# Fewer matmuls for a per-batch rank product: high and low halves side by side, one group at a time, in a five-engine fp32 kernel

## The reference

```python
def _L0_cond_ref(x, adapter_mapping, W, b, lora_As, lora_Bs):
    base_out = jnp.einsum('bti,oi->bto', x, W) + b
    A = lora_As[adapter_mapping]      # (128, 512, 16)
    Bm = lora_Bs[adapter_mapping]     # (128, 16, 512)
    lora_h = jnp.einsum('bti,bir->btr', x, A)
    lora_out = jnp.einsum('btr,bro->bto', lora_h, Bm)
    return base_out + lora_out * SCALING

x = x + _L0_ffn_ref(_L0_cond_ref(x, ...), W_gate, W_up, W_down)   # silu(gate) * up, 1376 wide, then down
x = x + _L1_ffn_ref(_L1_cond_ref(x, ...), ...)                    # two routed low-rank layers
```

## Time and profile before

| what | value |
|---|---|
| three runs, median (lowest to highest) | 981.73 us (980.36 to 982.88) |
| the profiled execution, device time | 981.22 us |
| its span in the trace | 979.5 us |
| PE busy | 972.1 us (99%) |
| DVE / ACT / POOL busy | 586.0 / 464.5 / 276.9 us |

### The profile page before, as it was taken

How to read it: one execution, slowest core, us unless ns; L and a number is a source line. 1 busy time by engine, 2 the same in 40 slices (tenths; PEclk the granted TensorE clock), 3 DMA queues, 4 the chain that set the end, 5 groups by cost and what they waited for, 6 DMA issues and landing times.

```text
span 979.5 us, 14271 instructions
## 1 busy us (share of the span) xinstructions
PE 972.1 (99%) x4723; PEld 822.1 (84%) x4723; DVE 586.0 (60%) x970; ACT 464.5 (47%) x855; POOL 276.9 (28%) x284
## 2 busy tenths in 40 slices
PE   9999999999999999999999999999999999999998
PEld 7888888888888888888888888888888899898986
DVE  4545487876992432685423398333278488786862
ACT  4646476655742333571333383233357264545342
POOL 5363524654300721400522230261140460000000
PEclk9999999999999999999999999999999999999999
DMA  7899868686968866877886777987688650616132
GB/s 239 269 362 321 265 232 300 243 295 243 369 237 296 295 195 193 278 235 263 278 278 195 234 246 249 322 280 194 194 275 314 236 194 22 236 37 223 65 108 86
DMA packets 131123, 230.14 MB, mean 235 GB/s; under 512 B 29798, under 2 KB 29799, under 8 KB 130539
## 3 DMA queue, kind: packets, MB, share of 16 engines
q1 hardware_dynamic: 126720, 216.35, 66.4%
q0 software_dynamic: 4192, 12.87, 3.6%
q10 hardware_dynamic: 138, 0.01, 0.0%
HBM read 165.74 MB, written 63.44 MB: 234 GB/s over the span
## 4 chain that ended last, share of the span: by engine, by line
PE 87%; SPq 5%; DVE 2%; DMA 2%; issue 2%; ACT 1%; ACTq 0%; DVEq 0%
PE bank L1951 87%; SPq L597 3%; DMA x_raw<-in_x 1%; PE bank L2114 1%; SPq L583 1%; DMA c<-c_scratch 1%; SPq L588 0%; DMA a_raw<-in_a_cols 0%; SPq L664 0%; DVE xa_lo L1502 0%; ACT c_out L1076 0%; SPq L596 0%; ACT dt L1102 0%; SPq L772 0%; DVE hg L1762 0%
## 5 line engine op out<-in xcount | busy, mean ns | idle before, releaser
L1951 PE MATMUL bank<-cop_hi,wring 128*128 128x512 f32 x1234 | 380.9, 389 | 0.0
L1951 PEld LDWEIGHTS bank<-cop_hi,wring 128*128 128x128 f32 x1234 | 231.6, 188 | 48.8 <-DVE v L1590 0.4
L1951 PE MATMUL bank<-cop_lo,wring 128*128 128x512 f32 x616 | 239.7, 389 | 0.0
L1951 PE MATMUL bank<-op_hi,wring 128*128 128x512 f32 x560 | 173.8, 389 | 0.0
L1590 DVE TENSOR_TENSOR v<-bank,p7s 128x512 f32<-128x512 f32 x44 | 30.4, 691 | 194.0 <-PE bank L1951 193.9
L1951 PEld LDWEIGHTS bank<-cop_lo,wring 128*128 128x128 f32 x616 | 115.6, 188 | 24.0
L1951 PEld LDWEIGHTS bank<-op_hi,wring 128*128 128x128 f32 x560 | 105.1, 188 | 22.0 <-DMA wring<-wd_scratch 0.2
L1951 PE MATMUL bank<-op_lo,wring 128*128 128x512 f32 x280 | 108.9, 389 | 0.0
L1176 ACT ACTIVATE s<-bank 128x512 f32<-128x512 f32 x44 | 26.3, 597 | 112.6 <-PE bank L1951 112.6
L1576 DVE TENSOR_TENSOR op_lo<-h,op_hi 128x512 fp32r<-128x512 f32 x100 | 72.6, 743 | 3.7 <-ACT op_hi L1133 3.6
L909 POOL TENSOR_TENSOR h_t<-h,h 128x512 f32<-128x512 f32 x20 | 27.1, 1356 | 160.8 <-DVE h L1612 160.8
(11 more groups left out here) (243 smaller groups left out, 1925.8 us busy)
## 6 DMA issues: line engine op xcount, KB each, us to landing
wring<-wgu_scratch SPq DMA_DIRECT2D x231, 256.0 KB, 3.1
wring<-wd_scratch SPq DMA_DIRECT2D x140, 256.0 KB, 5.5
wgu_scratch<-wring SPq DMA_DIRECT2D x77, 256.0 KB, 3.5
c_scratch<-c_out POOLq DMA_DIRECT2D x32, 256.0 KB, 3.3
c<-c_scratch SPq DMA_DIRECT2D x32, 256.0 KB, 4.7
xs_raw<-x_scratch SPq DMA_DIRECT2D x16, 512.0 KB, 5.2
out<-res SPq DMA_DIRECT2D x32, 256.0 KB, 2.1
x_raw<-in_x SPq DMA_DIRECT2D x14, 512.0 KB, 5.8
```

Source lines behind the costliest of these rows:

```text
L1951: return e.matmul(out_ap, lhs, rhs, start=start, stop=stop, skip_group_check=True)
```

## The change

The weights of a group now hold, for each of two halves of 4 batches, 64 columns of high and 64 columns of low part of A (`a_both`; the order low, high, high, low lets one copy write all the high ones, and `a_place` puts the batches to suit). The moving operand is the high and low part of 128 tokens side by side, 256 columns (`xa` holds both). One matmul per chunk and half gives all four partial products, so the rank product has 2 x 2 x 4 = 16 matmuls of 256 columns. Each group has a bank of its own. Three of the four quarter results have to be added: ACT turns those that lie on the other 64 partitions (`lora_turn`, two copies into `h_turned`), DVE adds twice and then scales and masks (`lora_in`, three operations that depend on one another, 256 elements wide), ACT and DVE make high and low part per group. DVE's `a_lo` is two half-size operations per group. `h_turned` is cleared once at the start.

The first two tiles are woven anew by groups. `load_x(3)` moves from t = 1 to t = 0 on SP, `load_down` from t = 0, 1 to t = 1, 2. The 14 down steps stand four places later, in tiles 2 to 5. In tile 6 three `cop_split` stand ahead of the closings instead of six, and one follows each closing.

```diff
-    a_hi = work("a_hi", [NG, KC, P], F32R)
-    a_lo = work("a_lo", [NG, KC, P], F32R)
+    a_both = work("a_both", [NG, KC, 2 * P], F32R)
...
-    xa_hi = [work(f"xa_hi{s}", [KC, TOK], F32R) for s in range(2)]
-    xa_lo = [work(f"xa_lo{s}", [KC, TOK], F32R) for s in range(2)]
+    xa = [work(f"xa{s}", [2, KC, TOK], F32R) for s in range(2)]
...
+    h_turned = sb("h_turned", [NG, 2, GT // 2], F32, w_region + 8 * ROW)
...
-    c_ring = [("h", t, 0, "dve") for t in range(NT)]
+    c_ring = [("h", t, g, "dve") for t in range(NT) for g in range(NG)]
...
-    ring_bank_at = [3, 3] + [n % 4 for n in range(2, len(c_ring))] + [n % 4 for n in range(len(l_ring))]
+    ring_bank_at = [3] * 4 + [(n + 2) % 4 for n in range(len(c_ring) - 4)] + [n % 4 for n in range(len(l_ring))]
...
-    d_at = [KC + 1 + n for n in range(N_EARLY)]
+    d_at = [2 * KC + 1 + n for n in range(N_EARLY)]
...
+    HB, HR = GB // 2, P // 2
+    def a_views(g, b, at_col):
+        n = b.stop - b.start
+        return (a_both[:, g, :, at_col:at_col + n * R].rearrange("p k (b r) -> p k b r", b=n),
+                a_raw[:, g, b, :].rearrange("p b (k r) -> p k b r", k=KC))
+    def a_place(b):
+        return (b + HB) % GB
+    def h_n(t, g=NG - 1):
+        return NG * t + g + 1
+    def h_bank(t, g):
+        return ring_bank("h", t, g)[:, :].rearrange("p (w h c) -> p w h c", w=2, h=2)
+    def by_turn(ap):
+        return ap.rearrange("p (w c) -> p w c", w=2)
...
# SP
-            if t == 1:
+            if t == 0:
                 for ks in x_parts(3):
                     load_x(3, ks)
-            if t < 2:
-                load_down(t)
+            if 0 < t < 3:
+                load_down(t - 1)
...
# ACT
+        def lora_turn(t, g):
+            both = h_bank(t, g)
+            e.wait_ge(pe_ring, ring_full("h", t, g))
+            if t == 0:
+                e.wait_ge(dve_chain, ZEROS + 1)
+            else:
+                e.wait_ge(*ring_freed("h", t - 1, g))
+            e.activation(h_turned[0:HR, g, 0, :], both[HR:P, 0, 0, :], ACT.Copy).then_inc(h_turned_done, 1)
+            e.activation(h_turned[HR:P, g, 1, :], both[0:HR, 1, 0, :], ACT.Copy).then_inc(h_turned_done, 1)
...
-        lora_in(0)
-        turn_a(1)
+        turn_b(0)
+        for g in range(NG):
+            lora_turn(0, g)
+            lora_hi(0, g)
+        turn_a(1, (0,))
+        lora_turn(1, 0)
...
-        for m in close_order(0):
-            close_c(0, m)
+        close_c(0, 0)
+        turn_a(1, (1,))
+        close_c(0, 1)
+        lora_hi(1, 0)
+        close_c(0, 2)
+        close_c(0, 3)
+        turn_b(1)
+        lora_turn(1, 1)
+        split_x(2, (0, 1))
+        lora_hi(1, 1)
+        split_x(2, (2, 3))
...
-            for q, i in cop_due(t)[:6]:
+            ahead = 3 if t == NT - 2 else 6
+            for q, i in cop_due(t)[:ahead]:
                 cop_split(0, q, i)
             for r, m in enumerate(close_order(t)):
                 close_c(t, m)
                 for n in d_due(t, r):
                     down_hi(n)
-            for q, i in cop_due(t)[6:]:
-                cop_split(0, q, i)
+                if t == NT - 2:
+                    for q, i in cop_due(t)[ahead + r:ahead + r + 1]:
+                        cop_split(0, q, i)
+            if t == NT - 1:
+                for q, i in cop_due(t)[ahead:]:
+                    cop_split(0, q, i)
...
# DVE
-            e.scalar_tensor_tensor(
-                out=h_masked[:, :].rearrange("p (g c) -> p g c", g=NG),
-                in0=ring_bank("h", t, 0)[:, :].rearrange("p (g c) -> p g c", g=NG), scalar=SCALING,
-                in1=own_batch[:, :].unsqueeze(1).to_broadcast([P, NG, GT]),
-                op0=ALU.mult, op1=ALU.mult).then_inc(dve_freed, 1)
+            linked(e.tensor_tensor(by_turn(mine), both[:, :, 0, :], h_turned[:, g, :, :], ALU.add))
+            e.wait_ge(dve_chain, links[0])
+            linked(e.tensor_tensor(by_turn(mine), both[:, :, 1, :], by_turn(mine), ALU.add))
+            e.wait_ge(dve_chain, links[0])
+            e.scalar_tensor_tensor(out=mine, in0=mine, scalar=SCALING, in1=own_batch[:, :],
+                                   op0=ALU.mult, op1=ALU.mult).then_inc(dve_freed, 1)
...
# PE
-            for g in range(NG):
-                e.wait_ge(a_lo_done, NG * t + g + 1)
+            e.wait_ge(a_lo_done, h_n(t, g))
+            for w in range(2):
+                at_tok = g * GT + w * GT // 2
+                first = P if w == 0 else 0
                 for k in range(KC):
-                    if g == 0:
+                    if g == 0 and w == 0:
                         e.wait_ge(x_lo, x_n(t, k))
-                    tok = slice(g * GT, (g + 1) * GT)
-                    done = mm3(bank[:, tok], a_hi[:, g, k, :], a_lo[:, g, k, :],
-                               xa_hi[s][:, k, tok], xa_lo[s][:, k, tok], k == 0, k == KC - 1)
+                    done = mm(by_turn(bank[:, w * GT:(w + 1) * GT]), a_both[:, g, k, first:first + P],
+                              xa[t % 2][:, :, k, at_tok:at_tok + GT // 2], k == 0, k == KC - 1)
...
-        lora_out(0)
-        lora_in(1)
+        lora_out_half(0, 0)
+        lora_in(1, 0)
+        lora_out_half(0, 1)
         e.wait_ge(c_closed, c_turn(0, 0))
-        for k in range(KC):
-            cond_base(1, KC - 1, k)
-        lora_out(1)
+        cond_base(1, KC - 1, 0)
+        cond_base(1, KC - 1, 1)
+        lora_in(1, 1)
+        cond_base(1, KC - 1, 2)
+        cond_base(1, KC - 1, 3)
+        lora_out_half(1, 0)
+        lora_out_half(1, 1)
```

More of the change, by code:

```diff
@@ L102, in build @@
     lh_lo = [work(f"lh_lo{s}", [TOK], F32R) for s in range(2)]
-    xa_hi = [work(f"xa_hi{s}", [KC, TOK], F32R) for s in range(2)]
-    xa_lo = [work(f"xa_lo{s}", [KC, TOK], F32R) for s in range(2)]
+    xa = [work(f"xa{s}", [2, KC, TOK], F32R) for s in range(2)]
+    xa_hi, xa_lo = ([xa[s][:, half, :, :] for s in range(2)] for half in range(2))
     h_masked = work("h_masked", [TOK], F32)
@@ L390, in build @@
     IDENT, MASK, LATER, EXPERT = 3, 6, 8, 9
-    ZEROS, ROWS = 1, 4
+    ZEROS, ROWS = 1, 5
     def x_parts(t):
@@ L1047, in split_w0, with turn_a @@
             e.activation(w0_hi[:, k, :], w0_raw[:, k, :], ACT.Copy).then_inc(w0_hi_done, 1)
-        def turn_a(t):
-            for g in range(NG):
+        def turn_a(t, gs=range(NG)):
+            for g in gs:
                 if (t, g) == (0, 1):
@@ L1533, in lora_in @@
-            e.wait_ge(lh_hi_done, t + 1)
-            e.tensor_tensor(lh_lo[t % 2][:, :], h_masked[:, :], plain(lh_hi[t % 2][:, :]),
+            if t > 0:
+                e.wait_ge(lh_lo_done, h_n(t - 1, g))
+            linked(e.tensor_tensor(by_turn(mine), both[:, :, 0, :], h_turned[:, g, :, :], ALU.add))
[4 more added lines that the diff above has]
+                                   op0=ALU.mult, op1=ALU.mult).then_inc(dve_freed, 1)
@@ L1535, in lora_in, with lora_rest @@
+        def lora_rest(t, g):
+            tok = slice(g * GT, (g + 1) * GT)
+            e.wait_ge(lh_hi_done, h_n(t, g))
+            e.tensor_tensor(lh_lo[t % 2][:, tok], h_masked[:, tok], plain(lh_hi[t % 2][:, tok]),
                             ALU.subtract).then_inc(lh_lo_done, 1)
@@ L1796, in dve_program @@
         turn_a(0)
-        lora_in(0)
-        turn_a(1)
+        turn_b(0)
+        for g in range(NG):
+            lora_in(0, g)
+            lora_rest(0, g)
+        turn_a(1, (0,))
+        lora_in(1, 0)
+        turn_a(1, (1,))
+        lora_rest(1, 0)
+        turn_b(1)
+        lora_in(1, 1)
+        split_x(2, (0, 1))
+        lora_rest(1, 1)
+        split_x(2, (2, 3))
         for t in range(1, NT):
-            if t == 1:
-                split_x(2, (0, 1))
-            else:
+            if t > 1:
                 turn_a(t)
+                turn_b(t)
                 if t < NT - 1:
                     split_x(t + 1)
-            if t == NT - 1:
-                for n in range(7):
-                    gate_up_lo(n)
-                cop_begin(0, 1)
-            lora_in(t)
-            if t == 1:
-                split_x(2, (2, 3))
+                if t == NT - 1:
+                    for n in range(7):
+                        gate_up_lo(n)
+                    cop_begin(0, 1)
+                for g in range(NG):
+                    lora_in(t, g)
+                for g in range(NG):
+                    lora_rest(t, g)
             if t == NT - 2:
@@ L1993, in cond_base, with cond_lora @@
                 xa_hi[t % 2][:, k, :], xa_lo[t % 2][:, k, :], k == 0, False)
-        def cond_lora(t, m):
+        def cond_lora(t, m, g):
             s = t % 2
-            for g in range(NG):
-                tok = slice(g * GT, (g + 1) * GT)
-                done = mm3(c_banks(t)[m][:, tok], b_hi[s][:, g, m * P:(m + 1) * P], b_lo[s][:, g, m * P:(m + 1) * P],
-                           lh_hi[s][:, tok], lh_lo[s][:, tok], False, g == NG - 1)
-            done.then_inc(pe_acc, 1)
+            tok = slice(g * GT, (g + 1) * GT)
```

(17 more changed lines are left out.)

111 lines of the change are left out of this document (60 added, 51 removed).

## The result

The changed kernel takes 985.59 us (median of 7 runs, 984.54 to 986.82) beside 981.73 us before (7 runs, 980.34 to 982.88): 1.0044 times, 95% interval 1.0033 to 1.0055 (such a ratio is worked out from all the runs and is not the quotient of the two medians). It is slower by 0.4%, where 980.6 [976.5 to 984.5] was forecast. The profiled execution took 986.48 us, its span 984.8. Of all executions behind this document one, of the later version back_and_lora, took 1975.54 us, and its ratio leaves it out.

What follows compares the result with a forecast made beforehand. The path feeding tile 7 (SP's issues, load of c, splits), not PE alone, was taken to decide. PE's 7.7 us, mostly lost to two waits, left 0.1 to 0.7; 1.1 was taken: 981.22 to 980.1, median 980.6 [976.5 to 984.5].

Steps and rivals of the forecast that it cites:

- PE's part: Rank product: eight fewer matmuls a tile, 0.12 us apart, save 0.96 us a tile, 7.7 in eight tiles.
- rival C: Rank product: the two-run read is slower, at 0.228 us a matmul 6 us in all, 988 us; chance 0.04.
- Tiles 0 and 1: First two tiles: about 2 us of waits in place of 0.9, tile 2 starts 0.85 us earlier, bounds 0 and 2.8.
- SP's queue: SP's gathers and loads: tile 4's gathers 3.3 us earlier, near 61; load_c starts at 110.8 for 113.19.
- the landing of that store: Tile 5's last store, issued at about 114.3, lands after the median 5.5 us, so cop_hi starts at 119.8.
- rival B: Stores of tile 5 come late and hold ACT's first cop_split; at 12.0 us of landing 988 us; chance 0.11.
- floor: Behind load_c: the last store lands no sooner than c itself, 118.2, and not at 117.4.
- Rival E: Expansion of tile 7: PE's pause ahead of it costs speed, some 1.7 us, ending at 982.3; chance 0.05.
- D: The prediction's own forecast for the whole kernel, 978.8 to 983 us; chance 0.50.
- better half: Whole kernel: a saving of 1.1 us was taken, where the middle values gave 0.1 to 0.7 and the best case 2.6.
- The end of tile 7: From c's data to the last lh_lo 4.74 us, 1.35 more than before; PE waits 3 to 3.6 us.
- Rival A: Path ahead of tile 7 is not the bound, PE keeps its saving: 975.2 to 976.7 us, near part 978; chance 0.30.

Runs made afterwards that it cites:

- back_and_lora: Changed kernel with down steps and their reads in the old tiles and DVE's cop_begin(0, 1) behind lora_in(7): 982.17 beside 981.11 us, 1.0005.
- Experiment 13: Changed kernel with each early down step storing 128 of its 512 columns: 981.47 beside 981.14 us, 1.0013.
- Experiment 7: Changed kernel with POOL's sums of down weights behind lh_lo of tiles 2 and 4: 984.84 beside 981.23 us, 1.0033.
- Experiments 9 to 12: clear_path (981.52 us), and clear_path with stores behind the next tile's first gathers (983.11), later down steps (982.52), or a quarter of early store bytes (976.75).
- clear_path: Changed kernel with down steps and reads in old tiles, POOL's sums after DVE's lora operations, cop_begin(0, 1) behind lora_in(7): 981.52 beside 981.23 us, 1.0001.
- filler: Changed kernel with ten unused matmuls of 512 columns ahead of the expansion of tile 7: 989.8 beside 981.23 us, 1.0082.
- experiments 3, 10 and 11: Changed kernel with tile 5's stores ahead of the first c load (986.27 us); clear_path with stores behind the next first gathers (983.11), or later down steps (982.52).
- experiment 14: clear_path with three down steps a tile in place of four, the last two stores behind c: 980.5 beside 981.74 us, 0.9991.
- steps_back: Changed kernel with the 14 down steps and the reads of down weights back in their old tiles: 981.98 beside 981.37 us, 1.0008.
- sums_clear: The run of Experiment 7, changed kernel with POOL's sums behind lh_lo of tiles 2 and 4: 984.84 beside 981.23 us, 1.0033.
- old_steps_late: Kernel before with only the changed kernel's late down steps, reads of down weights and early x read: 986.98 beside 981.37 us, 1.0061.
- stores_first: Changed kernel with SP issuing the three stores of tile 5 ahead of the first load of c: 986.27 beside 981.37 us, 1.0051.
- after_few_bytes: The run of Experiment 13, changed kernel with a quarter of the columns in the early down stores: 981.47 beside 981.14 us, 1.0013.
- lora_first: Changed kernel with DVE's cop_begin(0, 1) behind the lora operations of tile 7: 983.82 beside 981.37 us, 1.0027.
- old_lora_first: Kernel before with DVE's cop_begin(0, 1) behind the lora operations of tile 7: 980.69 beside 981.23 us, 0.9997.

## Why the prediction was wrong

**PE's part: right.** 0.12 apart, 16 a tile, 15.72 us a tile without waits. The two-run read costs nothing, so rival C fell.

**Tiles 0 and 1: within the bounds, smaller.** Tile 2 starts at 40.49 for 39.9 forecast and 40.71 before: 0.2 us are saved, not 0.85.

**SP's queue: right.** Gathers of tile 4 at 61.22 (near 61), `load_c` at 110.53 (110.8), the last of the three stores issued by 113.27 for 114.3.

**The failed step: the landing of that store.** The sum took the median, 5.5 us, and set the first `cop_hi` to 119.8. It landed 10.9 us after its issue and `cop_hi` started at 124.27. That is rival B, which the prediction knew, with its place and its price (it decides "from 119.9 on", "each us later is a us lost"), and gave 0.11. Its price holds: `cop_hi` is 124.27 - 119.9 = 4.4 us late, and beside the same kernel with a quarter of the bytes (first `cop_hi` 119.42) the gate product is 146.51 - 140.73 = 5.8 us later, of which the half speed below is 1.1 to 1.5. The reason not to take the median was in view: its 5.5 is of 14 stores, and these three stood behind 1 MB of `c`, in a stretch whose windows I had not read: in the kernel before the DMA engines are busy for 0.84 to 1.00 of the time from 40 to 120. The row's own range went to 12.0, and the store that counts is the last of three: the last ones of a tile had taken 5.6 to 11.7. Experiment 13 shows that the bytes are the term: with a quarter of them in the stores the first `cop_hi` starts at 119.42.

The Trainium skill's rule in DMA: Bandwidth & Descriptors, on queues, rings and completion order, by which the increment waits for that engine's earlier writes, was used for a floor. The trace agrees, since the stores land behind `c`, and it shows how little the floor says: the loads of `c` had landed 4.3 to 5.7 us after their issues of 110.5 to 111.9, thus by 118, and the last store behind them at 124.2.

**The second missing term: the pause.** Rival E was priced at 1.7 us and given 0.05, as if it were an alternative. It hangs on B and D alike, because both forecast a pause of 3 us ahead of the expansion. It came, with 4.33 - 2.87 = 1.46 us. The Trainium skill, TensorE: Matmul & The Clock Gate, warns, in its table of why this matters for your kernels, of idle gaps after which the clock halves; the trace agrees for this pause (clock 0.64) and not for the one of 2.38 us at the start of the same tile, behind which nothing slowed. The reason given against E, that a wait of 0.9 us left no mark, said nothing of one of 3. The two terms, 4.4 + 1.5, on 980.1 give 986.0 for the 986.48 measured. In that agreement is some luck: 980.1 holds a gain of 1.1 us, where the middle values of the sum were 0.1 to 0.7 and no reason stands for the "better half", and rival B's 988 counts its 6.4 us with no gain at all. The gate product bears the 1.1 out: 146.51 - 4.4 - 1.5 = 140.6, 1.0 ahead of 141.61.

**A wait that was not forecast.** The prediction said that POOL's `down_sums` go with the steps and gave them no cost. They stretch DVE's small operations in tiles 3 and 4: 1.77 + 2.15 us of PE. The stretched ones read both operands from SBUF. The Trainium skill, GPSIMD Engine Reference, says in its Specifications that GpSimd shares its SBUF interfaces with VectorE, with contention for DVE instructions with two SBUF inputs; the trace agrees, 1.71 us for 0.42. Experiment 7 shows that these waits set the end by 1 us at most (1.0033 for 1.0044, intervals that overlap), since tile 7 waits for ACT anyway.

**The end of tile 7: right in its working.** From the arrival of `c` to the last `lh_lo` the sum had 4.74 us; 142.13 - 137.29 = 4.84 was measured. The 2.4 us wait for `c_out` and the 2.5 for `lh_lo` are where they were said to be, and smaller than the 3.5 and 3 to 3.6 forecast because PE itself came later than forecast by more than they did: it began tile 6 at 107.29 and not at 39.9 + 4 x 15.72 = 102.8.

**Rival A** would have needed an SP queue and rings with slack. Experiments 9 to 12 show why there was none: in clear_path the DMA share in tiles 2 to 5 is 0.92 to 1.06, and only fewer bytes let PE keep its saving.

What is open: whether `c` or other stores were ahead of the late ones in each DMA engine's work cannot be read from these views. Why the second group's gathers of tile 5 come 2.7 us later in clear_path than in the kernel before, with the same stores in the same tiles, and why the version with the filler took 3.6 us more behind tile 7, was not followed up.

## What to carry to other kernels

Where a transfer that somebody waits for is moved, price its landing by what is issued just ahead of it and by the DMA share of that stretch, not by the median of its kind; where several are waited for, by that of the last. A transfer issued far ahead shows in no wait how late it lands. When an engine gets 6% faster, look at the stage's DMA share: here, at 0.92 and more, it came to wait for bytes, and the three orders tried (experiments 3, 10 and 11) only chose who waits. A forecast that contains a pause of PE should hold a slow restart as a possible term: here it cost 1.2 to 2.9 us where it came. And when work moves, look at what it now lies beside on every engine: POOL's sums met DVE's small operations in tiles 3 and 4, with the steps back in tiles 2 and 3, and, tied behind `lh_lo`, in tile 4 of experiment 14.

## What the runs showed of the hardware

- A store of 512 KB behind 1 MB of loads and two such stores landed 10.9 us after its issue; with a quarter of the bytes in the stores, 6.3 at most; ahead of the loads, three such stores landed within 5.8 us, and the loads behind them took 8.8 to 9.5.
- In the changed kernel, of two pauses of PE of 2.4 and 2.5 us matmuls of 256 columns stood 0.21 apart for 3 us (granted clock 0.64 on the mean of the expansion) only after the second; after the first the base product ran at its usual distances. In steps_back a pause of 2.4 us was followed by twelve matmuls 0.12 apart and only then by twelve 0.21 apart.
- The length of the pause alone did not decide it. After 3.4 us in sums_clear (tile 7, from 127.88) and 3.0 us in filler (from 128.78) nothing slowed; after 3.9 us in clear_path and 4.1 us in old_steps_late it did. The same wait of 1.89 us in tile 4 left no mark in the changed kernel, in stores_first and in after_few_bytes, and was followed by half-speed matmuls in lora_first and filler (19.19 and 19.36 us for the tile, for 17.87).
- DVE's fp32 operations of 256 elements with both inputs in SBUF took up to 1.7 us beside POOL's `TENSOR_TENSOR` of 512, four times their 0.42. POOL's own took 1.30 to 1.46.
- Behind the three stores, SP's issues of `c` took 1.1 to 1.5 us each instead of 0.43. Stores just ahead are not needed for that: in old_lora_first two issues of `c` took 1.0 and 1.5 us (at 111.43 and 112.52) with none there. What holds an issue up is not shown.
